# Turning h behind both aggregations, with the products of gT first, in a max-of-relations graph layer

## The reference, cut to what matters

```
h   = relu(layernorm(x))
A   = [adj, adj, shifted, adj^T, adj^T, shifted^T, eye]        # shifted acts on the batch as identity of the nodes here
HW  = einsum('bnf,rfo->rbno', h, W[:, :F]) + (W_edges . W[:, F:])[:, None, None, :]
out = max_r einsum('rbnm,rbmo->rbno', A, HW) + b
x   = x + out
```

## Time and profile before

| | |
|---|---|
| median of three runs | 202.38 us (202.1 to 202.52) |
| the profiled execution, its own time | 202.54 us |
| its span, first to last instruction | 200.6 us |
| TensorE busy in the span | 194.4 us |
| VectorE, ScalarE, GpSimd busy | 170.4, 155.4, 119.1 us |
| TensorE's granted clock | 1.00 throughout |

### The profile page before, as it was taken

One profiled execution on the slowest core, in us unless ns is written; L12 is line 12 of the kernel. 1 busy time (PEld: TensorE's weight loads), 2 busy tenths in 40 slices (PEclk: granted clock), 3 DMA queues, 4 the chain that ended last, 5 costly groups with the idle time before them and its releaser, 6 DMA issues.

```text
span 200.6 us, 3385 instructions
## 1 busy us (share of the span) xinstructions
PE 194.4 (97%) x900; PEld 148.7 (74%) x900; DVE 170.4 (85%) x415; ACT 155.4 (77%) x426; POOL 119.1 (59%) x166
## 2 busy tenths in 40 slices
PE   6998999999999999999999999999999999999991
PEld 6556467678788787878878787877878787887871
DVE  3468969999988998899988998989998999868764
ACT  4788889996999659992999839994799929991220
POOL 5113334576685766658496566659486566967601
PEclk9999999999999999999999999999999999999999
DMA  5999999969996989987897978979897998651041
GB/s 175 326 319 369 377 337 361 308 210 334 372 332 182 283 251 276 320 300 201 296 288 236 317 261 260 341 226 244 258 298 278 283 254 228 163 132 28 22 83 52
DMA packets 33746, 51.06 MB, mean 254 GB/s; under 512 B 1872, under 2 KB 11328, under 8 KB 33728
## 3 DMA queue, kind: packets, MB, share of 16 engines
q1 hardware_dynamic: 31152, 46.53, 70.1%
q0 software_dynamic: 2304, 4.20, 12.0%
q10 hardware_dynamic: 272, 0.13, 0.2%
HBM read 46.65 MB, written 4.19 MB: 253 GB/s over the span
## 4 chain that ended last, share of the span: by engine, by line
PE 88%; DVE 3%; SPq 3%; DMA 3%; issue 1%; DVEq 0%
PE bank_p L929 12%; PE bank_p L930 10%; PE bank_p L931 10%; PE bank_gT L876 6%; PE bank_gT L867 6%; PE bank_gT L870 6%; PE bank_g L890 6%; PE bank_g L893 6%; PE bank_g L899 6%; PE bank_p L919 3%; PE bank_p L805 3%; DMA w_sb<-in_W_dram 3%; PE bank_gT L844 2%; PE bank_g L853 2%; PE bank_g L930 2%; PE bank_g L929 2%
## 5 line engine op out<-in xcount | busy, mean ns | idle before, releaser
L354 POOL TENSOR_TENSOR a_lo<-adj_sb,a_hi 128x512 fp32r<-128x512 f32 x28 | 35.7, 1290 | 27.5 <-issue 14.0
L696 DVE TENSOR_TENSOR best<-bank_p,best 128x512 f32<-128x512 f32 x47 | 32.5, 691 | 4.4 <-PE bank_p L931 3.0
L455 ACT ACTIVATE a_hi<-adj_sb 128x512 fp32r<-128x512 f32 x56 | 34.5, 628 | 0.0
L347 POOL TENSOR_TENSOR o_sb<-best,x_bias 128x512 f32<-128x512 f32 x15 | 19.4, 1297 | 25.3 <-DVE aT_lo L648 15.0
L464 ACT ACTIVATE aT_hi<-adjT_sb 128x512 fp32r<-128x512 f32 x56 | 34.5, 623 | 0.0
L361 POOL TENSOR_TENSOR aT_lo<-adjT_sb,aT_hi 128x512 fp32r<-128x512 f32 x26 | 33.1, 1292 | 0.0
L497 ACT ACTIVATE gT_hi<-bank_gT 128x512 fp32r<-128x512 f32 x16 | 9.5, 591 | 28.4 <-PE bank_gT L876 27.6
L693 DVE SCALAR_TENSOR_TENSOR best<-bank_p,c_col,best 128x512 f32<-128x512 f32 x32 | 23.9, 747 | 1.4 <-ACT best L518 0.5
L476 ACT ACTIVATE h<-x_sb,shift,rstd 128x128 f32<-128x128 f32 x60 | 24.7, 489 | 0.3 <-DVE shift L634 0.3
L929 PE MATMUL bank_p<-hT_hi,w_hi 128*128 128x512 f32 x48 | 19.7, 410 | 0.0
L930 PE MATMUL bank_p<-hT_hi,w_lo 128*128 128x512 f32 x48 | 18.7, 390 | 0.0
(11 more groups left out here) (131 smaller groups left out, 470.5 us busy)
## 6 DMA issues: line engine op xcount, KB each, us to landing
adj_sb<-in_adj_dram SPq DMA_DIRECT2D x15, 1024.0 KB, 7.2
adjT_sb<-in_adjT_dram SPq DMA_DIRECT2D x15, 1024.0 KB, 6.3
x_bias<-in_biasT_dram SPq DMA_DIRECT2D x16, 256.0 KB, 7.5
x_bias<-in_xT_dram POOLq DMA_DIRECT2D x16, 256.0 KB, 7.5
x_sb<-in_x_dram SPq DMA_DIRECT2D x15, 256.0 KB, 8.4
out_dram<-o_sb SPq DMA_DIRECT2D x15, 256.0 KB, 5.7
adj_sb<-in_adj_dram SPq DMA_DIRECT2D x4, 256.0 KB, 4.4
adjT_sb<-in_adjT_dram SPq DMA_DIRECT2D x4, 256.0 KB, 4.9
```

What stands on the lines that cost most here:

```text
L354: nc.gpsimd.tensor_tensor(a_lo[q][:, c, :], adj_sb[q][:, c, :], a_hi[q][:, c, :].bitcast(F32), ALU.subtract).then_inc(alo_last_ready, 1)
L455: nc.scalar.activation(a_hi[q][:, c, :], adj_sb[q][:, c, :], ACT.Copy, accum_out=sums[q][:, 0, c:c + 1]).then_inc(ahi_ready, 1)
L696: op = nc.vector.tensor_tensor(best[q][:, :], product, best[q][:, :], ALU.max)
```

## The change

For batches 4 to 14 (`late`), `turn_h` stands behind `aggregate`: in a leader next to `turn_sums`, in a follower next to the burst of four matmuls on 32 rows. The products of gT come first. A leader runs the six passes of gT's two products, then the three products of hT, then the burst, which ends gT's products and begins g's, then g's products. A follower runs the burst first, then the products in the order gT, gT, hT, hT, hT, g, g; the second of gT goes into bank_gT, none into bank_g. So the aggregation over adjT behind a follower waits for no maximum, and the one over adj waits for the follower's first `take_best`.

ScalarE splits hT behind h and h_hi of the next batch. The splits of adjT for the next leader move from behind the follower's `begin_best` to the start of the follower's turn in the loop. VectorE's order is written anew: in a leader aT_lo, gT_lo, a_lo of the next batch, h_lo of the next, hT_lo, g_lo, variance, maximum; in a follower scale_and_shift, aT_lo, gT_lo, variance, a_lo of the next, hT_lo, h_lo of the next, g_lo, scale_and_shift, maximum. GpSimd's and SyncE's code is as it was. Batches 0 to 3 and 15 keep their order on TensorE.

```diff
@@ scalar, in the loop over b
-                if leads(b):
+                if late(b):
+                    if follows(b):
+                        std_of(b + 1)
                     split_adjT(b + 1)
                 split_gT(b)
-                split_hT(b)
-                if 2 <= b < B - 2:
-                    std_of(b + 2)
+                if not late(b):
+                    split_hT(b)
+                    if 2 <= b < B - 2:
+                        std_of(b + 2)
                 if b + 1 < B:
                     make_h(b + 1)
-                    if not leads(b):
-                        split_h(b + 1)
+                    split_h(b + 1)
+                if late(b):
+                    if follows(b) and b + 2 < B:
+                        std_of(b + 2)
+                    split_hT(b)
                 split_g(b)
...
@@ vector
+            for b in range(PAIRED, B, 2):
+                split_adjT_lo(b)
+                split_gT_lo(b)
+                split_adj_lo(b + 1)
+                split_h_lo(b + 1)
+                split_hT_lo(b)
+                split_g_lo(b)
+                if b + 2 < B:
+                    variance(b + 2)
+                for i in range(1, NPROD):
+                    take_best(b, i)
+                b = b + 1
+                if b < B - 1:
+                    scale_and_shift(b + 1)
+                split_adjT_lo(b)
+                split_gT_lo(b)
+                if b < B - 1:
+                    variance(b + 2)
+                    split_adj_lo(b + 1)
+                split_hT_lo(b)
+                if b < B - 1:
+                    split_h_lo(b + 1)
+                split_g_lo(b)
+                if b < B - 1:
+                    scale_and_shift(b + 2)
+                    for k in range(1, NPROD):
+                        take_best(b, k, tail_order[k], tail_bank[tail_order[k]])
...
@@ tensor
+            def products_lead(b):
+                pe.wait_ge(best_done, b * NBEST)
+                pe.wait_ge(gTlo_ready, b + 1)
+                for i in range(NH, NPROD - 2):
+                    passes(i, bank_of[i][:, 0:N], start=True)
+                for i in range(NH):
+                    product(b, i)
+                pe.wait_ge(crow_ready, 1)
+                pe.wait_ge(glo_ready, b + 1)
+                for i in range(NH, NPROD - 2):
+                    add_sums(b, i, bank_of[i], stop=True).then_inc(prod_psum, 1)
+                for i in range(NPROD - 2, NPROD):
+                    add_sums(b, i, bank_of[i], start=True)
+                for i in range(NPROD - 2, NPROD):
+                    product(b, i)
+            def products_follow(b):
+                pe.wait_ge(best_done, b * NBEST)
+                pe.wait_ge(gTlo_ready, b + 1)
+                pe.wait_ge(sumsT_ready, turn_of(b) + 1)
+                pe.wait_ge(crow_ready, 2)
+                for i in range(NH, NPROD):
+                    add_sums(b, i, tail_bank[i], start=True)
+                for i in tail_order:
+                    if i == 0:
+                        pe.wait_ge(hTlo_ready, b + 1)
+                    if i == NPROD - 2:
+                        pe.wait_ge(glo_ready, b + 1)
+                    passes(i, tail_bank[i][:, 0:N], start=ORDER[i] in H_RELS, stop=True).then_inc(prod_psum, 1)
...
-                turn_h(b)
+                if not late(b):
+                    turn_h(b)
                 if b < FIRST:
                     aggregate_whole(b)
                 else:
                     aggregate(b)
+                if late(b):
+                    turn_h(b)
                 if not follows(b):
                     turn_sums(b)
```

More of the change, by code:

```diff
@@ L127, in gnn_kernel @@
         bank_of = bank_p + [bank_g]
+        tail_order = tuple(range(NH, NPROD - 2)) + tuple(range(NH)) + (NPROD - 2, NPROD - 1)
+        tail_bank = dict(zip(tail_order, (bank_p[3], bank_gT, bank_p[0], bank_p[1], bank_p[2], bank_p[4], bank_p[5])))
         last_banks = ((bank_p[5], bank_gT), (bank_g, bank_p[0]))
@@ L222, in follows, with late @@
             return b >= 1 and leads(b - 1)
+        def late(b):
+            return PAIRED <= b < B - 1
         def turn_of(b):
@@ L489, in split_hT @@
                 if b >= 1:
-                    act.wait_ge(prod_psum, (b - 1) * NPROD + NH)
+                    act.wait_ge(prod_psum, (b - 1) * NPROD + NH + 2)
                 nc.scalar.activation(hT_hi[:, :], bank_h[:, 0:N], ACT.Copy).then_inc(hThi_ready, 1)
@@ L517, in begin_best @@
                     act.wait_ge(out_ready, b - 1)
+                if late(b) and follows(b):
+                    nc.scalar.activation(best[q][:, :], tail_bank[tail_order[0]][:, 0:N],
+                                         ACT.Copy).then_inc(best_begun, 1)
+                    return
                 nc.scalar.activation(best[q][:, :], bank_of[0][:, 0:N], ACT.Identity,
@@ L584, in _ @@
                     std_of(b + 2)
-                if b + 1 < B and not leads(b):
+                if b + 1 <= PAIRED:
                     split_adjT(b + 1)
@@ L681, in rows_of_c, with take_best @@
                                                op1=ALU.add).then_inc(crow_ready, 1)
-            def take_best(b, i):
+            def take_best(b, k, i=None, bank=None):
                 q = b % 2
+                i = k if i is None else i
                 r = ORDER[i]
-                if i == 1:
+                if k == 1:
                     dve.wait_ge(best_begun, b + 1)
                 else:
-                    dve.wait_ge(best_done, b * NBEST + i - 1)
-                dve.wait_ge(prod_psum, b * NPROD + i + 1)
-                product = bank_of[i][:, 0:N]
+                    dve.wait_ge(best_done, b * NBEST + k - 1)
+                dve.wait_ge(prod_psum, b * NPROD + k + 1)
+                product = (bank or bank_of[i])[:, 0:N]
                 if r in H_RELS:
@@ L759, in _ @@
             scale_and_shift(3)
-            for b in range(2, B):
-                if b + 2 < B:
-                    variance(b + 2)
+            for b in range(2, PAIRED):
+                variance(b + 2)
                 split_adjT_lo(b)
@@ L766, in _ @@
                 split_hT_lo(b)
-                if b + 2 < B:
-                    scale_and_shift(b + 2)
[L769 to L777, removed]
+                scale_and_shift(b + 2)
[11 more added lines that the diff above has]
+                split_g_lo(b)
+                if b + 2 < B:
+                    variance(b + 2)
+                for i in range(1, NPROD):
+                    take_best(b, i)
+                b = b + 1
[4 more added lines that the diff above has]
+                if b < B - 1:
+                    variance(b + 2)
+                    split_adj_lo(b + 1)
+                split_hT_lo(b)
+                if b < B - 1:
+                    split_h_lo(b + 1)
+                split_g_lo(b)
+                if b < B - 1:
+                    scale_and_shift(b + 2)
+                    for k in range(1, NPROD):
+                        take_best(b, k, tail_order[k], tail_bank[tail_order[k]])
+                else:
+                    for i in range(1, NPROD - NLAST):
+                        take_best(b, i)
             b, q = B - 1, (B - 1) % 2
@@ L801, in turn_h @@
                 pe.wait_ge(h_ready, b + 1)
-                if b >= 1:
+                if late(b):
+                    pe.wait_ge(best_done, b * NBEST)
+                elif b >= 1:
                     pe.wait_ge(best_done, (b - 1) * NBEST + 1)
@@ L864, in aggregate_T @@
                 pe.wait_ge(gTlo_ready, b)
+                if follows(b - 1) and late(b - 1):
+                    pe.wait_ge(best_done, (b - 1) * NBEST + 1)
                 for c in range(C):
@@ L881, in aggregate @@
                 q = b % 2
-                pe.wait_ge(best_done, b * NBEST)
+                if not (follows(b - 1) and late(b - 1)):
+                    pe.wait_ge(best_done, b * NBEST)
                 if b == FIRST:
@@ L986, in _ @@
                     aggregate(b)
+                if late(b):
+                    turn_h(b)
                 if not follows(b):
                     turn_sums(b)
[L989 to L993, removed]
+                if late(b) and leads(b):
+                    products_lead(b)
+                elif late(b):
+                    products_follow(b)
+                else:
+                    for i in range(NH):
+                        product(b, i)
+                    begin_products(b)
+                    for i in range(NH, NPROD - NLAST * int(b == B - 1)):
+                        product(b, i)
             for i in range(2):
```

## The result

The changed kernel takes 209.72 us (median of five runs, 209.46 to 209.96), the one before 202.19 in the same number of runs: 1.0366 times as long, with an interval of 1.035 to 1.0382. The profiled execution took 209.96 us with a span of 208.1.

The account below looks back on a forecast made before the run. The prediction took a fully busy TensorE as the bound: five leader waits of 0.9 us less 0.3 saved give +4.2 on the median of 202.4, so 206.6 us, with an 8-in-10 range of 201.8 to 209.3.

Parts of the forecast that it names:

- What bounds the kernel: TensorE is busy 23.08 of 23.08 us in a pair; only less work or a new wait there moves the time.
- The place and the cause: PE waits ahead of turn_sums for POOL's part_sums in leaders 6, 8, 10, 12 and 14, 0.9 us each.
- When DVE is free: DVE's maxima end 1.9 us into the follower and 2.45 into the next leader, 1.95 without shift held up.
- The lateness of the chain: In a leader, sums through aT_lo, finish and part_sums are ready at 5.99 against 5.90 wanted: late by 0.1 us.
- The term that failed: In leaders, part_sums beside DVE's two a_lo and h_lo grows by 0.77 us, so PE waits 0.87, taken as 0.9.
- the upper bound: At turn_sums, h_lo holds up the last of part_sums' four instructions too: wait of 1.5 us a leader, about 210.
- my case: Five leaders wait 0.9 us at turn_sums, less 0.3 saved: 206.6 us, own range 203.7 to 209.9, chance 0.60.
- the faster cases: Rival: part_sums gets through or DVE is earlier, PE never waits: 202.1 us, at most 201.9 by chain prices; chance 0.20.
- PE's work: Transposes beside other short matmuls stop slowing the passes behind them: 0.3 us saved over batches 4 to 14.
- The lower bound: PE's saving is at least nothing, if the slow spacing moves on to gT's products; at most 0.45 us.
- The hT chain: hT_lo is ready 0.1 us before PE asks in a leader; rival that it comes late: 203.2 us, chance 0.05.
- The other edits at nothing: Moved adjT splits, their load, SyncE's queue and add_bias cost nothing; the cover is 0.1 to 1.5 us.

Follow-up runs that it names:

- the run with the sums ahead: The changed kernel, with GpSimd making part_sums ahead of finish in a leader: 205.29 us, 1.0128 of the kernel before.
- the early shift: The changed kernel, with a follower's second scale_and_shift behind hT_lo and ahead of h_lo instead of behind g_lo: 209.21 us, 1.0337 of the kernel before.
- the run with two edits: The changed kernel, with part_sums ahead of finish and hT_lo ahead of h_lo in a leader: 202.37 us, 1.0012 of the kernel before.

## Why the prediction was right or wrong, point by point

*What bounds the kernel.* Right: PE was full, and a new wait on it was the whole result.

*The place and the cause.* Right: five leaders from batch 6 on, at the turn of sums, behind part_sums; batch 4 (11.85 us) and the followers as they were.

*When DVE is free.* Right. I had 2.45 us into the leader with shift held up; it was 2.49, and 1.92 without (I had 1.95). finish was put at 3.8 and started at 3.89. The lateness of the chain, 0.1 in the sum, measured 0.2: with nothing held up the sums came where they were put (PE turned them at 6.03, the sum had 5.99), but PE asks for them at 5.81 in the timeline and not at 5.90.

*The term that failed: "By the rows of batch 14 part_sums grows by 0.77: PE waits 0.87".* The growth was 2.12 - 0.88 = 1.24; with the lateness of 0.2 that is nearly all of the wait, 1.48 as the leader's growth. In batch 14 two instructions of DVE stood beside part_sums, and the first copy had already begun when the first of them did; here three stood ready, and the first copy, too, had to wait. I had named the third, h_lo, as what makes 1.5, and kept it for the upper bound. It was the case, though by another way: I had h_lo hold the last of the four, and the last was the one that went free. 5 x 1.48 is 7.4, where I took 4.5. That put 206.6 where 209.7 was measured, 0.4 above the upper end of the range for 8 in 10; my case's own range, to 209.9, held it, and I had cut it short to make room for the faster cases.

*PE's work.* Wrong by 0.3: the second aggregation lost its slow spacing (2.73 instead of 2.78), but the passes behind the turns and the burst took 5.54 instead of 5.47. The lower bound, nothing, was right, and so was its reason, that the slow spacing moves on.

*The hT chain.* Covered in the five leaders, as forecast, but the wait for the sums itself covers it there by 1.48 us more. In batch 4, which has no such wait, it came late by some 0.1 us: PE began the hT products 0.1 behind the end of hT_lo, the same distance as in the run with the sums ahead.

```profile
64.74 0.68 DVE L675 TENSOR_TENSOR hT_lo<-bank_p,hT_hi 128x512 fp32r<-128x512 f32 x1
...
65.53 0.47 PE L981 MATMUL bank_p<-hT_hi,w_hi 128*128 128x512 f32 x1
```

Batch 4 took 11.85 here, and 11.70 and 11.92 in two runs with hT_lo ahead of h_lo; what sets it there is open. So the cover was thin: with the sums ahead, one held h_lo brought the chain out, at 0.5 us a leader.

*The other edits at nothing.* Right as far as the list of waits shows: from batch 4 on PE waits for no load, no split of adjT and no copy.

## What to carry to other kernels

Where an order on one engine has been arranged around another engine, ask of each instruction that is moved what will now stand beside it, not only what it waits for: here the same instructions of DVE cost nothing or 7 us by their neighbours. When small instructions have to pass a row of long ones that hold a shared path, count one hold for each long one that stands ready (here 0.39 to 0.46 us each, by the growth of part_sums beside one, two and three), and take the count from the new order, not from the nearest case in the old trace. A chain that is just in time can have a second one beside it: shortening the one that the trace names (the early shift) bought nothing, and shortening the other as well put a long instruction in the way and took 2.3 us more.

## What the runs showed that I had not expected

That shift would be held up was in the prediction, but as one long instruction of over 1 us. An instruction of 128 x 4 elements took 0.74 us beside POOL's a_lo, and 0.16 otherwise. What no part of the prediction had: in the leaders of the changed kernel POOL's own four subtractions took 2.81 a pair where they took 2.55 a pair in the followers and 2.53 in the run with two edits:

```profile
88.18 0.85 POOL L346 DMA_DIRECT2D x_bias<-in_xT_dram  x1
88.78 2.81 POOL L361 TENSOR_TENSOR a_lo<-adj_sb,a_hi 128x512 fp32r<-128x512 f32 x2
91.28 2.81 POOL L368 TENSOR_TENSOR aT_lo<-adjT_sb,aT_hi 128x512 fp32r<-128x512 f32 x2
...
102.40 2.55 POOL L361 TENSOR_TENSOR a_lo<-adj_sb,a_hi 128x512 fp32r<-128x512 f32 x2 [2.51 <-issue]
```

Here the first begins 0.25 us before the record of the transfer's issue (L346) ends; in the run with two edits there is a gap of 0.23. It goes with this distance in every run: each of the four takes 1.54 to 1.58 where the first begins some 0.24 before that end, 1.40 to 1.43 where it is about 0.1 before, and 1.27 to 1.33 where it begins with the end or behind it. Why was not tried; it costs PE nothing here.
